# A graph network layer with routed experts: block rows of the tail loaded up to seven steps ahead, last stores on another queue, collects spread wider

## The chip, the cores and the metric

One Trainium2 chip, one of its cores. The engines are TensorE (PE, with its weight loads as PEld), VectorE (DVE), ScalarE (ACT), GpSimd (POOL) and SyncE (SP, which here only issues transfers). The metric is the time of one execution on the device in microseconds, as the median of several runs.

## The reference, cut to what matters

The layer has 6250 nodes of 256 float32 values and 200000 edges sorted by destination.

```python
edge_index = jnp.stack([src, dst])
xn = _layernorm(x, axis=-1)
x = x + gnn(xn, edge_index, W, att_src, att_dst, bias) + mix(xn[None], ...)[0]
x = x + ffn(_layernorm(x, axis=-1)[None], gamma, beta, Wr, br, W1, b1, W2, b2)[0]
```

`gnn` is graph attention with four heads: every edge weighs its source's row by a softmax over the edges of one destination, and the rows are summed per destination. `mix` is linear attention over all nodes followed by a two-layer product with a gelu. `ffn` is what the change touches: each node picks two of eight experts by its logits, each expert is 256 -> 512 -> 256 with a gelu between, and the two results are summed with the softmax of the two logits as weights:

```python
logits = xn @ Wr + br
top_vals, top_idx = jax.lax.top_k(logits, 2)
w = jax.nn.softmax(top_vals, axis=-1)
for e in range(8):
    h = jax.nn.gelu(xn @ W1[e] + b1[e], approximate=False)
    y = y + (h @ W2[e] + b2[e]) * w_full[..., e, None]
```

## The kernel before, in words

**Steps.** All engines walk through one plan of 211 numbered steps, each engine with its own program and semaphores between them. A step up to 168 (`NS` = 169) carries one group of 1024 edges: GpSimd gathers the source rows into `rows_g`, VectorE builds a one-hot matrix `pick_e` (two places, 128 x 8 x 128 float32 each) and weighs the rows, TensorE multiplies them (`sums`, L2366) and signals `summed`. Beside this, each step carries pieces of the other work. From step 169 on only that other work is left; this is the tail. SyncE's loop runs with a lag of five passes, so that its step `c` is named like the others' steps.

**Routing.** The 49 tiles of 128 nodes are finished in the order 48 down to 0. Tile t is routed at step `route_at[t]` (tile 1 at 169, tile 0 at 170): its row is normed, its logits are computed (L2460, L1841), its two experts chosen, and its rows written to `sent_dram`, where each expert has a region. Tiles 48 to 24 are scattered by GpSimd. Tiles 23 to 0 are sorted by expert with a product (`sort`, L2479), stored in `sorted_dram` (`keep_sorted`, L1416) and then handed out to the regions, two experts to a piece (`hand_out`, L1430, on SyncE). The tiles 10, 5, 1 and 0 are rushed: half of their pieces is handed out by ScalarE (`hand_out_rest`, L2212 to L2214), for tile 1 in ScalarE's step 179 and for tile 0 in its step 180.

**Sets and blocks.** The tiles form four sets: 48 to 24, 23 to 10, 9 to 5, and 4 to 0. When a set is routed, `table` writes which blocks of 128 rows it has and whose expert each is (`table_ready`). The sets have 42, 43, 17 and 17 blocks. At the end of the last three sets the regions are filled up with zeros (`fills`, L1454: eight transfers of 384 KB), which must come after the hand-outs before it and ahead of those of the next tile. `fill_at` gives the step, 176 for the last set; its second term, the end of the hand-outs before, is below that.

**One block** is one job. The jobs of the third set stand at steps 167 to 183, those of the last set at 184 to 200. Job n at step s goes through: load of its rows by SyncE at step s-3 (`block_inputs`, L1384) into one of the two places of `xe` (the buffer `xin`), after the turn of job n-2; turn by TensorE at step s-1 (`turn_x`, L2376); taken to `xnT` by ScalarE (L2144), which at step s also copies the expert's first weights to `W1_now` (L2156); up product at step s (L2404, sixteen matmuls); gelu by ScalarE (L2171); down product at step s+2 (`down`, L2442 for the bias and then L2444, eight matmuls); copy from PSUM into one of the two places of `ys` (the buffer `xn`) by VectorE at step s+3 (`result`, L1793), which must wait until the store of job n-2 has landed (`ys_out`); and store to `set_dram`. Up to job step 168 the store is SyncE's at step s+3 (L1393); from 169 on (`LATE`) it is ScalarE's at step s+4 (L2227). In TensorE's program a step reads: turn of the next job, sums, sort products, down product of the job two steps back (after VectorE's copy of the job before that one), up product.

**The end of a tile.** When all blocks of a span of sets (the first two sets, then each by itself) are stored, each tile is collected: GpSimd gathers its two result rows per node from `set_dram` (`collect`, L1577, two gathers of 128 KB), SyncE reloads the kept sum for tiles from 9 on (`x1_again`, L1463, at step `final_at[t]`), VectorE adds both with their shares (`combine`, L1977 and L1980, at `final_at[t]` + 2, for the last set + 4), and SyncE stores the rows of the output (`give`, L1468, one step later). There are six places for this (`TAIL_SPOTS`) in the freed `rows_g`: collect and reload of the f-th tile wait for the sum of the tile six before. `final_at` begins at 171 and gives two tiles to each step, up to 193 for tile 5 (summed at 195); the last set's five tiles stand at 204 and 205.

Of the kernel before, what the change touches and what calls it, by code (L numbers as in the profile page):

```python
# [10 lines left out]
P = 128  # L11
# [24 lines left out]
WINDOWS = 8  # L36
NEAR = 6
CUTS = (24, 10, 5)
CLOSED = (1, 2, 3)
TAIL_RATE = 3  # L40
COLLECT_RATE = 2
TAIL_SPOTS = 6
SPARE_F = 8
PADDED = 1 << 14
# [4 lines left out]
TURNED = 14  # L49
XR = 14  # L50
SORT_BUFS = 8
BY_TWO = 2


def gps_layer(nc, x, xT, src_cols, dst_cols, W_turned, att_cols, inner_cols, src, dst, gnn_W, att_src, att_dst, gnn_bias, w_qkv, b_qkv, kln_g, kln_b, vln_g, vln_b,
# [3 lines left out]
    NT = -(-N // P)  # L59
# [15 lines left out]
    NE, _, H = W1.shape  # L75
# [10 lines left out]
    sent_dram = nc.dram_tensor("sent_dram", (NE * REGION + max(SPARE, SPARE_F) * P, D), F32).ap()  # L86
# [14 lines left out]
    SETS = tuple(zip((FULL,) + tuple(c - 1 for c in CUTS), CUTS + (0,)))  # L101
# [4 lines left out]
    NS = NG - COUNTED  # L106
    LATE = NS
# [6 lines left out]
    def steps_until(t):  # L114

        return min(NS, NG - int(NG * math.sqrt(P * t / N)) + 2)

    mix_first = PAIRS + 5
    mix_at, route_at, table_at, final_at = {}, {}, [], {}
    for t in range(FULL, -1, -1):  # L120
        mix_at[t] = mix_first + FULL - t
    for t in range(FULL, -1, -1):
        at = max(steps_until(t), mix_at[t] + 8)
        if t == 0:
            at = max(at, pair_at[-1] + 2)
        if t < FULL:
            at = max(at, route_at[t + 1] + 1)
        if t + 3 <= FULL:
            at = max(at, route_at[t + 3] + (4 if t + 3 >= CUTS[0] else 6))
        if t + 2 < CUTS[0]:  # L130
            at = max(at, route_at[t + 2] + 3)
        if any(t == hi for hi, _ in SETS[1:]):
            at = max(at, table_at[-1] - 4, mix_at[0] - 3)
# [20 lines left out]
    SORTED = tuple(range(SETS[0][1] - 1, -1, -1))  # L154
    HANDS = NE // BY_TWO
    RUSHED = tuple(t for t in SORTED if any(t == lo for _, lo in SETS[1:]) or route_at[max(t - 1, 0)] < route_at[t] + HANDS and t - 1 in (lo for _, lo in SETS[1:]))
# [4 lines left out]
        piece_at_step[c] = waiting[:now] + [(t, k) for t in RUSHED if route_at[t] + 9 == c for k in range(HANDS // 2)]  # L161
        waiting = waiting[now:]
    handed_at = {t: c for c, gone in piece_at_step.items() for t, _ in gone}
    fill_at = {x: max(route_at[SETS[x][1] + 1] + 7, handed_at[SETS[x][1] + 2] + 1) for x in CLOSED}
    assert all(fill_at[x] <= min(c for c, gone in piece_at_step.items() if SETS[x][1] + 1 in dict(gone)) for x in CLOSED)
    downs_dram = nc.dram_tensor("downs_dram", (3 * NE, D), BF16).ap()
    sorted_dram = nc.dram_tensor("sorted_dram", (SORT_BUFS, 3 * P, D), F32).ap()
    set_dram = [nc.dram_tensor(f"set_dram{w}", (span_blocks[w] * P, D), F32).ap() for w in range(len(spans))]

    job_at, job_step, mix_number, last_job = {}, {}, {}, []  # L170
# [4 lines left out]
    for z in range(len(SETS)):  # L175
        at = max(table_at[z] + (7 if z else 4), max(job_at) + (1 if z else 4))
        for k in range(set_blocks[z]):
            job_at[at + k] = (len(job_step), "block", z, k)
            job_step[len(job_step)] = at + k
        last_job.append(len(job_step) - 1)  # L180
    xe_count = {}
    for n, kind, _, _ in job_at.values():
        same = [m for m, other, _, _ in job_at.values() if m <= n and m % 2 == n % 2]
        kinds = {m: other for m, other, _, _ in job_at.values()}
        xe_count[n] = sum(1 for m in same if kinds[m] == "block")
    tiles_in = [range(hi, lo - 1, -1) for hi, lo in SETS]
    span_tiles = [[t for x in range(a, b + 1) for t in tiles_in[x]] for a, b in spans]
    for w, (_, z) in enumerate(spans):
        ends = z == len(SETS) - 1
        at = max([job_step[last_job[z]] + (4 if ends else 5)] + [c + 1 for c in final_at.values()])  # L190
        for f, t in enumerate(span_tiles[w]):
            final_at[t] = at + f // (TAIL_RATE if ends else COLLECT_RATE)
    assert spans[-1][0] == spans[-1][1] and min(final_at.values()) >= NS
    final_number = {t: f for f, t in enumerate(final_at)}
    assert max(final_at[t] for t in final_at if t not in tiles_in[-1]) < job_step[last_job[-1]] + 4
# [12 lines left out]
    turn_number = {}  # L208
# [25 lines left out]
    with ExitStack() as ctx:  # L234
# [7 lines left out]
        ident = sb("ident", [P, P])  # L242
# [843 lines left out]
        _, loop_sem = last_phase.enter_context(phase())  # L1086
        loop_marks = []

        def loop_stage(ph):
            def sem(name):  # L1090
                loop_marks.append(loop_sem("loop_" + name))
                return loop_marks[-1]

            rows_g = sb("rows_g", [P, RING, EG, HW_], c=ph)
            pick_e = sb("pick_e", [P, SLOTS, EG, P], c=ph)
# [44 lines left out]
            blk_expert = sb("blk_expert", [1, P], I32, c=ph)  # L1140
            cuts = sb("cuts", [1, SORT_BUFS, 2, NE], I32, c=ph)
            xe, ys = xin, xn
            freed = acc[:, SETS[0][1]:NT].rearrange("p t c -> p (t c)")
            cells = lambda lo, n: freed[:, lo:lo + n]
            bias_parts = cells(H // 2, D // 2).bitcast(BF16)
# [81 lines left out]
            ps_pick, ps_sum, ps_xT, ps_hT, ps_up, ps_small = psA[0], psB, psA[1], psC[0], psC[1], psD[1]  # L1227
# [8 lines left out]
            local_in, window_in = [sem(f"local_in{r}") for r in range(AHEAD)], [sem(f"window_in{r}") for r in range(WINDOWS)]  # L1236
# [2 lines left out]
                                 "ph_ready", "summed", "added", "ids_set"))  # L1239
            xT_in, xe_in, ys_out = ([sem(f"{n}{u}") for u in range(2)] for n in ("xT_in", "xe_in", "ys_out"))  # L1240
            base_in = [sem(f"base_in{v}") for v in range(4)]
            b_given_in, b_split_ready, b_split_out, bias_in, inner_bias_in, bias_of_ready = (sem("b_" + n) for n in ("given_in", "split", "split_out", "in", "inner_in", "of"))
            up_done, hb_ready, gelu_done, h_turned, hT_ready, down_done, ys_ready = (sem("j_" + n) for n in (
                "up_done", "hb_ready", "gelu_done", "h_turned", "hT_ready", "down_done", "ys_ready"))
            x_turned, xT_taken, weights_taken = sem("x_turned"), sem("xT_taken"), sem("weights_taken")
# [36 lines left out]
            def jobs_with(s):  # L1282
                return job_at[s] if s in job_at else None
# [15 lines left out]
            def sort_number(t):  # L1299
                return SETS[0][1] - 1 - t  # L1300

            def handed_by(t):

                return 16 * BY_TWO * (sort_number(t) + 1)

# [9 lines left out]
            def on_sync(sp):  # L1315
# [50 lines left out]
                def block_inputs(n, x, k):  # L1366
                    b, u = first_block[x] + k, n % 2
                    sp.wait_ge(table_ready, 2 * (x + 1))
                    at = sp.value_load(blk_row[0:1, b:b + 1], min_val=0, max_val=NE * REGION // P + SPARE_F - 1)
                    if k == 0:  # L1370
                        sp.wait_ge(ys_ready, NT)
                        for w in range(3):
                            sp.wait_ge(sent[w], 32 * scattered(w))
                        if x:
                            for piece in range(HANDS):
                                sp.wait_ge(handed[piece], handed_by(SETS[x][1]))
                        if filled_by(x):
                            sp.wait_ge(fills_out, filled_by(x))
                        sp.wait_ge(spare_out, 16 * SPARE_F)
                        sp.wait_ge(x1_first, 16 * FIRST_KEPT)  # L1380
                        sp.wait_ge(x1_out, 16 * (NT - FIRST_KEPT - SETS[0][1]))
                    if ("job", n - 2) in turn_number:
                        sp.wait_ge(x_turned, turn_number[("job", n - 2)] + 1)
                    sp.dma_start(xe[:, u], sent_dram[bass.ds(at * P, P)]).then_inc(xe_in[u], 16)  # L1384

                def store(n, kind, a, k):
                    u = n % 2
# [20 lines left out]
                def keep_sorted(t):  # L1408
                    n = sort_number(t)
                    sp.wait_ge(xT_taken, turn_number[("high", t)] + 1)  # L1410
                    if n == 0:
                        sp.wait_ge(tails_out, 16 * SORT_BUFS)
                    if n >= SORT_BUFS:
                        for k in range(HANDS):
                            sp.wait_ge(handed[k], handed_by(t + SORT_BUFS))
                    sp.dma_start(sorted_dram[n % SORT_BUFS, 0:2 * P].rearrange("(k p) n -> p k n", p=P), sorted_home[n % 2][:]).then_inc(sorted_out[n % 2], 16)  # L1416

# [52 lines left out]
                with sp.If(general_value(sp) == 0):  # L1470
# [7 lines left out]
                    for s in range(STEPS + LAG):  # L1478
# [17 lines left out]
                        c = s - LAG  # L1496
                        for i in range(NT):
                            if i // 2 - 2 == c:
                                kv_inputs(i)
                        job = jobs_with(c + 3)  # L1500
                        if job and job[1] == "block" and job[0] >= NT + 2:
                            block_inputs(job[0], job[2], job[3])
                        job = jobs_with(c - 3)
                        if job and (job[1] == "mix" or c - 3 < LATE):
                            store(*job)
                        job = jobs_with(c + 3)
                        if job and job[1] == "block" and job[0] < NT + 2:
                            block_inputs(job[0], job[2], job[3])
                        job = jobs_with(c + 2)
                        if job and job[1] == "mix":  # L1510
                            mix_inputs(job[0], job[2])
                        job = jobs_with(c + 1)
# [617 lines left out]
            def on_scalar(act):  # L2130
# [151 lines left out]
                with act.If(general_value(act) == 0):  # L2282
# [8 lines left out]
                    for s in range(STEPS):  # L2291
# [47 lines left out]
                        for x in range(len(SETS)):  # L2339
                            if table_at[x] == s:  # L2340
                                exponentials(x)
                        if s - 4 >= LATE and jobs_with(s - 4):
                            store(*jobs_with(s - 4))

            def on_tensor(pe):
# [22 lines left out]
                    last.then_inc(summed, 1)  # L2368

                def turn_x(n):  # L2370
                    u = n % 2
                    pe.wait_ge(xe_in[u], 16 * xe_count[n])
                    if turn_number[("job", n)] > 0:
                        pe.wait_ge(xT_taken, turn_number[("job", n)])
                    for c in range(KT):
                        last = pe.transpose(ps_xT[:, c * P:(c + 1) * P], xe[:, u, c * P:(c + 1) * P], ident[:])  # L2376
                    last.then_inc(x_turned, 1)

                experts = {}
# [1369 lines left out]
```

## Time and profile before

| | us |
|---|---|
| median of 3 runs | 2117.38 (2115.78 to 2124.63) |
| the profiled execution | 2116.04 |
| its span, first to last instruction | 2114.3 |
| TensorE busy | 1766.4 |
| VectorE busy | 1595.4 |
| GpSimd busy | 1454.6 |
| ScalarE busy | 1214.1 |

The mean granted clock of TensorE over the span is 0.902 of its full speed. The shares of busy time are averages over stages of different kinds: the edge loop takes the first nine tenths of the span, and the tail from about 1890 us on has other limits. Rows are therefore read by stretch. Times in rows are in microseconds from the start of the span. Matmul ends are modelled, so the starts of matmuls are the sharper marks. A tile name in a row is the program's name of the buffer, which may hold other data by then: `xin` holds block rows, `xn` finished blocks, `rows_g` in the tail the collected and kept rows, `acc` tables in cells that have become free.

### The profile page before, as it was taken

How to read it: one execution, taken by the hardware profiler on the slowest of the kernel's cores; microseconds unless marked ns; L12 is line 12 of the kernel's file. 1: busy time of each engine (PE TensorE's matmuls, PEld its weight loads, DVE VectorE, ACT ScalarE, POOL GpSimd, SP SyncE). 2: the span in 40 equal slices, each digit the busy share in tenths (PEclk: the TensorE clock that was granted, in tenths of full speed). 3: DMA queues.
4: the chain of work that ended last, by engine and by line, in shares of the span. 5: the costliest groups of instructions: out<-in, count | busy, mean ns of one | idle time of the engine just before them, and what ended most of it. 6: DMA issues, size and time to landing. Idle time of an engine off the chain costs nothing. (4 is left out here: it accounts for less than half of the span.)

```text
span 2114.3 us, 40584 instructions
## 1 busy us (share of the span) xinstructions
PE 1766.4 (84%) x10047; PEld 1433.6 (68%) x10048; DVE 1595.4 (75%) x3938; ACT 1214.1 (57%) x2310; POOL 1454.6 (69%) x1586
## 2 busy tenths in 40 slices
PE   8499999678677777777788989889998999997684
PEld 6367777556555565555677777767877888885574
DVE  7678888567677777779888888979986998865341
ACT  4433333235454554444877787868865898855252
POOL 3277777777777777777766777766777777755451
PEclk9799999888787878778999999999999999998897
DMA  9676665686666666666776777876777778847772
GB/s 333 150 189 173 173 175 154 189 283 184 172 181 180 179 181 180 167 171 165 202 199 195 219 215 210 235 227 170 196 223 226 209 210 203 215 122 231 218 217 70
DMA packets 289175, 411.77 MB, mean 195 GB/s; under 512 B 108855, under 2 KB 211519, under 8 KB 285226
## 3 DMA queue, kind: packets, MB, share of 16 engines
q0 software_dynamic: 74208, 206.08, 36.4%
q1 hardware_dynamic: 194520, 185.22, 29.3%
q10 hardware_dynamic: 20210, 17.79, 2.9%
q8 instruction: 90, 1.47, 0.3%
q14 instruction: 147, 1.20, 0.2%
HBM read 354.61 MB, written 90.98 MB: 211 GB/s over the span
## 5 line engine op out<-in xcount | busy, mean ns | idle before, releaser
L1555 POOL DMA_INDIRECT rows_g<-node_table,src_all x1347 | 1282.6, 952 | 469.9 <-issue 407.9
L2366 PE MATMUL psB<-rows_g,pick_e 128*128 128x260 f32 x2704 | 747.4, 438 | 142.3 <-issue 120.0
L2366 PEld LDWEIGHTS psB<-rows_g,pick_e 128*128 128x128 f32 x2704 | 582.4, 221 | 266.8 <-issue 161.3
L1730 DVE TENSOR_TENSOR rows_g<-rows_g,psD 128x2048 f32<-128x2048 f32 x169 | 384.8, 2277 | 0.0
L2138 ACT ACTIVATE pick_n<-local_row 128x1024 bf16<-128x1024 bf16 x169 | 178.6, 1057 | 174.7 <-PE psA L2355 161.2
L2404 PEld LDWEIGHTS psC<-xnT,W_now 128*128 128x128 f32 x1904 | 233.8, 194 | 9.2 <-ACT W_now L2156 2.6
L2404 PE MATMUL psC<-xnT,W_now 128*128 128x128 f32 x1904 | 234.3, 277 | 1.6 <-ACT W_now L2156 1.6
L1701 DVE TENSOR_TENSOR pick_e<-psD,slot_all 128x1024 f32<-128x1024 f32 x169 | 203.4, 1204 | 0.1
L2134 ACT ACTIVATE local_row<-local_row,minus_id 128x1024 bf16<-128x1024 bf16 x169 | 191.6, 1134 | 15.8 <-DVE both_f L2040 8.7
L1793 DVE COPY xn<-psD 128x256 f32<-128x256 f32 x119 | 50.2, 422 | 179.3 <-DMA set_dram<-xn 97.0
L1577 POOL DMA_INDIRECT rows_g<-set_dram,places x98 | 95.0, 970 | 129.2 <-issue 86.0
L2355 PE MATMUL psA<-window,pick_n 128*128 128x24 bf16 x1352 | 59.5, 174 | 96.8 <-DVE psD L1711 51.3
L2355 PEld LDWEIGHTS psA<-window,pick_n 128*128 128x128 bf16 x1352 | 55.0, 99 | 119.5 <-issue 114.7
L2156 ACT ACTIVATE W_now<-W_f 128x1024 f32 x119 | 125.2, 1052 | 15.2 <-issue 13.9
L1719 DVE TENSOR_TENSOR p_both_e<-rows_g,psD 128x64 f32<-128x64 f32 x169 | 48.7, 288 | 110.2 <-DMA rows_g<-node_table,src_all 103.6
L2444 PE MATMUL psD<-W_f,hidT_more 128*128 x480 | 126.3, 408 | 0.0
L2444 PE MATMUL psD<-W_f,hidT 128*128 x472 | 120.9, 400 | 0.0
L2200 ACT ACTIVATE xdT<-psA 128x256 f32<-128x256 f32 (+1 forms) x49 | 18.9, 385 | 174.8 <-PE psA L2453 174.8
L2144 ACT ACTIVATE xnT<-psA 128x256 f32<-128x256 f32 x119 | 44.4, 373 | 114.7 <-PE psA L2376 98.5
L2444 PEld LDWEIGHTS psD<-W_f,hidT_more 128*128 128x128 f32 x480 | 90.5, 199 | 18.4 <-issue 0.9
L2444 PEld LDWEIGHTS psD<-W_f,hidT 128*128 128x128 f32 x472 | 87.0, 194 | 17.2 <-issue 0.4
L2492 PE MATMUL psC<-W_f,xnT 128*128 128x512 f32 (+1 forms) x196 | 90.0, 602 | 3.5 <-DMA xnT<-in_xT_dram 3.5
(387 smaller groups left out, 2924.0 us busy)
## 6 DMA issues: line engine op xcount, KB each, us to landing
local_row<-local_dram SPq DMA_DIRECT2D x169, 256.0 KB, 4.1
sent_dram<-sorted_dram SPq DMA_DIRECT2D x176, 128.0 KB
rows_g<-node_table,src_all POOLq DMA_INDIRECT x1347
xin<-sent_dram SPq DMA_DIRECT2D x119, 128.0 KB
xnT<-in_xT_dram SPq DMA_DIRECT2D x96, 128.0 KB
set_dram<-xn SPq DMA_DIRECT2D x87, 128.0 KB
sent_dram<-zero_dram SPq DMA_DIRECT2D x24, 384.0 KB
acc<-node_table SPq DMA_DIRECT2D x49, 128.0 KB
```

The lines of the kernel that those rows point to most:

```text
L1555: pool.indirect_dma_start(out=rows_g[:, r, j], out_offset=None, in_=node_table, in_offset=bass.IndirectOffsetOnAxis(ap=src_all[:, g, j:j + ...
L1577: pool.indirect_dma_start(out=final_home(f)[0][0:rows, c], out_offset=None, in_=set_dram[span_of[x]], in_offset=bass.IndirectOffsetOnAxis( ...
L1701: dve.tensor_tensor(pick_e[:, r], ids_here.unsqueeze(1).broadcast_to([P, EG, P]), slot_all[:, g].unsqueeze(2).broadcast_to([P, EG, P]), AL ...
L1730: dve.tensor_tensor(heads, heads, p_here.unsqueeze(3).broadcast_to([P, EG, HEADS, C]), ALU.mult).then_inc(ph_ready, 1)
L2134: act.activation(local_row[:, r], local_row[:, r], ACT.Abs, bias=minus_id[:]).then_inc(away_ready, 1)
L2138: act.activation(pick_n[:], local_row[:, r], ACT.Relu, bias=1.0, scale=-1.0).then_inc(pick_n_ready, 1)
L2156: act.activation(W1_now[:].rearrange("p k n -> p (k n)"), W1_f[:, bass.ds(experts[n], 1)].rearrange("p e k n -> p (e k n)"), ACT.Copy).the ...
L2355: last = pe.matmul(ps_pick[:, j * 6 * HEADS:(j + 1) * 6 * HEADS], pick_n[:, j * P:(j + 1) * P], window[:, w].rearrange("p k a -> p (k a)") ...
L2366: last = pe.matmul(ps_sum[s % 2][:, 0:AW], pick_e[:, s % SLOTS, j], rows_g[:, s % RING, j, 0:AW], start=(j == 0), stop=(j == EG - 1))
L2404: last = pe.matmul(inner_bank(n)[:, c * P:(c + 1) * P], W1_now[:, k, c * P:(c + 1) * P], xnT[:, u, k], start=(k == 0), stop=(k == KT - 1))
L2444: last = pe.matmul(ps_small[:, down_at], turned_rows(n, kind)[:, c], W2_f[:, bass.ds(e, 1), c], start=False, stop=(c == HK - 1))
L2492: last = pe.matmul((ps_up, ps_hT)[u][0:rows, :], xnT[:, u, k, 0:rows], wkv_s[:, k], start=(k == 0), stop=(k == KT - 1))
```

## The change

Three things change.

First, from job 139 (step 172) on, the block rows no longer go through the two places of `xe` but through eight places laid over `pick_e`, which the edge loop no longer needs. The first such load waits for the last `summed`; a load waits only for the turn of the job eight before. Jobs 139 to 143 are all loaded at step 169, the later ones of the third set seven steps ahead of their own, and those of the last set from step 180 on (four at 180, then one per step). Before, each was loaded three steps ahead. They use the semaphores of `window_in` further.

Second, the stores of the last set's blocks (steps 184 to 200) go from ScalarE at step s+4 to SyncE at step s+3. The third set's late stores (steps 169 to 183) stay on ScalarE.

Third, `final_at` of the tiles of the first three sets gives three tiles to two steps and not two to each, so that it runs to 199 and the sums to 201 (before 193 and 195), and the fill term is one step smaller: 175 for the last set, while those of the second and third stay at 116 and 137 by their other term.

```diff
-COLLECT_RATE = 2
+COLLECT_RATE = 3
+LATE_ROWS = 8
-    fill_at = {x: max(route_at[SETS[x][1] + 1] + 7, handed_at[SETS[x][1] + 2] + 1) for x in CLOSED}
+    fill_at = {x: max(route_at[SETS[x][1] + 1] + 6, handed_at[SETS[x][1] + 2] + 1) for x in CLOSED}
+    late_first = next(n for n, (at, kind) in enumerate((job_step[m], job_at[job_step[m]][1]) for m in range(len(job_step))) if kind == "block" and at >= NS + 3)
+    load_at = {n: at - 3 for n, at in job_step.items()}
+    for n in range(late_first, len(job_step)):
+        load_at[n] = max(job_step[n] - LATE_ROWS + 1, NS, route_at[0] + 10 if job_at[job_step[n]][2] == len(SETS) - 1 else 0)
-            final_at[t] = at + f // (TAIL_RATE if ends else COLLECT_RATE)
+            final_at[t] = at + (f // TAIL_RATE if ends else 2 * f // COLLECT_RATE)
...
+            late_rows = pick_e[:].rearrange("p r j n -> p (r j n)").rearrange("p (v c) -> p v c", v=LATE_ROWS)
+            late_spot = lambda n: (n - late_first) % LATE_ROWS
+            job_rows = lambda n: xe[:, n % 2] if n < late_first else late_rows[:, late_spot(n)]
...
+            late_in = window_in
+            def late_landed(n):
+                v = late_spot(n)
+                return 16 * (sum(1 for s in range(NS) if s % WINDOWS == v) + (n - late_first) // LATE_ROWS + 1)
... (block_inputs on SyncE)
+                    if n >= late_first:
+                        if n == late_first:
+                            sp.wait_ge(summed, NS)
+                        if n >= late_first + LATE_ROWS:
+                            sp.wait_ge(x_turned, turn_number[("job", n - LATE_ROWS)] + 1)
+                        sp.dma_start(job_rows(n), sent_dram[bass.ds(at * P, P)]).then_inc(late_in[late_spot(n)], 16)
+                        return
... (SyncE's loop)
-                        job = jobs_with(c + 3)
-                        if job and job[1] == "block" and job[0] >= NT + 2:
-                            block_inputs(job[0], job[2], job[3])
+                        for n in range(NT + 2, len(job_step)):
+                            if load_at[n] == c:
+                                block_inputs(n, *job_at[job_step[n]][2:])
                         job = jobs_with(c - 3)
-                        if job and (job[1] == "mix" or c - 3 < LATE):
+                        if job and (job[1] == "mix" or c - 3 < LATE or job[2] == len(SETS) - 1):
                             store(*job)
... (ScalarE's loop)
-                        if s - 4 >= LATE and jobs_with(s - 4):
+                        if s - 4 >= LATE and jobs_with(s - 4) and jobs_with(s - 4)[2] < len(SETS) - 1:
                             store(*jobs_with(s - 4))
... (turn_x on TensorE)
-                    pe.wait_ge(xe_in[u], 16 * xe_count[n])
+                    if n < late_first:
+                        pe.wait_ge(xe_in[n % 2], 16 * xe_count[n])
+                    else:
+                        pe.wait_ge(late_in[late_spot(n)], late_landed(n))
-                        last = pe.transpose(ps_xT[:, c * P:(c + 1) * P], xe[:, u, c * P:(c + 1) * P], ident[:])
+                        last = pe.transpose(ps_xT[:, c * P:(c + 1) * P], job_rows(n)[:, c * P:(c + 1) * P], ident[:])
```

## Rows read from the trace of the kernel before

**Rows 1.** Busy time by stretch: start:end, length, engines, granted clock, DMA share, GB/s.
```profile
1914.60:1940.00 25.40, 17.39 (x97) 13.84 (x96) 16.80 (x74) 10.09 (x26) 11.20 (x12) 0.83 0.64 183
1940.00:1963.40 23.40, 18.09 (x84) 14.93 (x83) 10.36 (x32) 8.49 (x17) 11.12 (x13) 0.75 0.87 294
...
2003.60:2035.10 31.50, 25.28 (x164) 21.77 (x163) 13.05 (x31) 17.05 (x42) 24.19 (x25) 1.00 0.84 253
...
2058.80:2089.30 30.50, 28.96 (x177) 24.52 (x176) 3.01 (x8) 15.60 (x39) 0.00 (x0) 1.00 0.20 66
```

**Rows 2.** Waits of TensorE, 1893 to 2092: in total, times, longest.
```profile
PE psD L2442 <- DVE xn L1793: 30.0, 15, 8.4
PE psD L2442 <- DVE logit_f L1841: 4.9, 1, 4.9
```

**Rows 3.** Waits of VectorE, 2003 to 2092.
```profile
DVE xn L1793 <- DMA set_dram<-xn: 56.9, 18, 4.5
```

**Rows 4.** Timeline of TensorE: start, duration, what, idle before it in brackets.
```profile
1893.49 0.28 PE L2442 MATMUL psD<-acc 24*128 24x256 bf16 x1
...
1897.63 0.28 PE L2442 MATMUL psD<-acc 24*128 24x256 bf16 x1
...
1956.78 0.39 PE L2442 MATMUL psD<-acc 24*128 24x256 bf16 x1 [4.48 <-DVE xn L1793]
...
1976.03 0.39 PE L2442 MATMUL psD<-acc 24*128 24x256 bf16 x1 [8.37 <-DVE xn L1793]
...
2003.56 0.28 PE L2442 MATMUL psD<-acc 24*128 24x256 bf16 x1
...
2028.31 0.28 PE L2442 MATMUL psD<-acc 24*128 24x256 bf16 x1
...
2087.02 0.28 PE L2442 MATMUL psD<-acc 24*128 24x256 bf16 x1 [0.77 <-DVE xn L1793]
```

**Rows 5.** Timeline of all engines, 2017 to 2025: one store and who needs it.
```profile
2017.03 0.38 PE L2376 MATMUL psA<-ident,xin 128*128 128x128 f32 x2
...
2018.66 0.33 ACTq L2227 DMA_DIRECT2D set_dram<-xn  x1
...
2023.46 0.42 DVE L1793 COPY xn<-psD 128x256 f32<-128x256 f32 x1 [3.83 <-DMA set_dram<-xn]
...
2024.04 0.28 PE L2442 MATMUL psD<-acc 24*128 24x256 bf16 x1 [1.88 <-DVE xn L1793]
```

**Rows 6.** TensorE grouped by line, 2003.56 to 2028.31, then 2028.31 to 2087.02.
```profile
L2442 PE MATMUL psD<-acc 24*128 24x256 bf16 x5 | 1.4, 276 | 3.7 <-DVE xn L1793 3.7
...
L2442 PE MATMUL psD<-acc 24*128 24x256 bf16 x13 | 3.6, 276 | 6.1 <-DVE xn L1793 5.9
```

**Rows 7.** Transfers by line, KB, median us to landing: 2003 to 2047, then 1936 to 1962.
```profile
rows_g<-x_dram SPq DMA_DIRECT2D x14, 128.0 KB, 3.8
...
rows_g<-x_dram SPq DMA_DIRECT2D x4, 128.0 KB, 7.7
```

**Rows 8.** Timeline of SyncE: the last set's fill.
```profile
1937.92 7.18 SPq L1454 DMA_DIRECT2D sent_dram<-zero_dram  x8
```

**Rows 9.** Timeline of VectorE: the second of tile 1's cut numbers.
```profile
1922.01 0.16 DVE L1877 CAST cuts<-acc 1x8 int32<-1x8 f32 x1
```

**Rows 10.** The chain that ended last, in order of time: start, duration, what.
```profile
1949.75 6.36 DMA set_dram<-xn
...
1957.17 3.71 PE psD L2444 x8
...
1999.70 1.92 PE psD L2444 x8
```

**Rows 11.** Timeline of ScalarE: the hand-outs of tile 1.
```profile
1966.76 6.35 ACTq L2214 DMA_DIRECT2D sent_dram<-sorted_dram  x4
```

**Rows 12.** Line L1577, 2003 to 2047: durations ns, first and last start, landings.
```profile
L1577 POOL DMA_INDIRECT rows_g<-set_dram,places x35: 942/946/1132, 2002.3 to 2045.7; - x35
...
DMA to landing us min/median/max: 2.7/3.9/4.9
```

More of the change, by code:

```diff
@@ L180, in gps_layer @@
         last_job.append(len(job_step) - 1)
+    late_first = next(n for n, (at, kind) in enumerate((job_step[m], job_at[job_step[m]][1]) for m in range(len(job_step))) if kind == "block" and at >= NS + 3)
+    load_at = {n: at - 3 for n, at in job_step.items()}
+    for n in range(late_first, len(job_step)):
+        load_at[n] = max(job_step[n] - LATE_ROWS + 1, NS, route_at[0] + 10 if job_at[job_step[n]][2] == len(SETS) - 1 else 0)
     xe_count = {}
     for n, kind, _, _ in job_at.values():
-        same = [m for m, other, _, _ in job_at.values() if m <= n and m % 2 == n % 2]
+        same = [m for m, other, _, _ in job_at.values() if m <= n and m % 2 == n % 2 and m < late_first]
         kinds = {m: other for m, other, _, _ in job_at.values()}
@@ L1241, in loop_stage @@
             base_in = [sem(f"base_in{v}") for v in range(4)]
+            late_in = window_in
+            assert LATE_ROWS == WINDOWS
+            def late_landed(n):
+                v = late_spot(n)
+                return 16 * (sum(1 for s in range(NS) if s % WINDOWS == v) + (n - late_first) // LATE_ROWS + 1)
             b_given_in, b_split_ready, b_split_out, bias_in, inner_bias_in, bias_of_ready = (sem("b_" + n) for n in ("given_in", "split", "split_out", "in", "inner_in", "of"))
@@ L1381, in block_inputs @@
                         sp.wait_ge(x1_out, 16 * (NT - FIRST_KEPT - SETS[0][1]))
+                    if n >= late_first:
[5 more added lines that the diff above has]
+                        return
                     if ("job", n - 2) in turn_number:
                         sp.wait_ge(x_turned, turn_number[("job", n - 2)] + 1)
-                    sp.dma_start(xe[:, u], sent_dram[bass.ds(at * P, P)]).then_inc(xe_in[u], 16)
+                    sp.dma_start(job_rows(n), sent_dram[bass.ds(at * P, P)]).then_inc(xe_in[u], 16)
                 def store(n, kind, a, k):
@@ L2370, in turn_x @@
                 def turn_x(n):
-                    u = n % 2
-                    pe.wait_ge(xe_in[u], 16 * xe_count[n])
+                    if n < late_first:
+                        pe.wait_ge(xe_in[n % 2], 16 * xe_count[n])
+                    else:
+                        pe.wait_ge(late_in[late_spot(n)], late_landed(n))
                     if turn_number[("job", n)] > 0:
```

## The prediction, made before the change was run

> **What bounds the kernel now.** I read the busy shares by stretch first [rows 1]. The edge loop ends at about 1890 us; the change touches nothing before that point except in name, since up to step 168 every load and store stands where it stood. So all of the gain or loss lies in the 220 us after it. There TensorE works 25.3 of 31.5 us from 2004 to 2035 with the DMA engines at 0.84, and 29.0 of 30.5 from 2059 to 2089 with them at a fifth. From 2089 on (25 us) only the last collects, sums and stores run. The reader should see that TensorE is the engine to follow until 2089 and that it has holes.
>
> Next, who makes the holes. TensorE's idle time ahead of the down product's first matmul (L2442) is 30.0 us on the copy of a finished block into `ys` (tile `xn`, L1793) and 4.9 us on a logit [rows 2]. That copy in turn waits for the store of the block two before it, because `ys` has two places: from 2003 to 2092 that is 56.9 us of VectorE's waiting, and nothing in it is for a block row or for the tail's gathered rows [rows 3]. A turn of block rows (L2376) nowhere waits for its load. So **the loads that are made earlier have nothing of their own to win**; what matters is what becomes free of them on SyncE, and how soon the stores land.
>
> An undisturbed step of one block takes 1897.63 - 1893.49 = 4.14 us, from one L2442 to the next [rows 4]. In the plan's count these are the starts of steps 169 and 170; step 184 starts at 2003.56, step 189 at 2028.31 and step 202, the last, at 2087.02.
>
> **How a store binds** [rows 5]. ScalarE's store of job k-4 comes in its step k, behind the take of the turned rows: turn at 2017.03, store issued at 2018.66, the copy that needed it at 2023.46 after 3.83 us of idling, and the down product at 2024.04, of whose lateness TensorE shows 1.88 us. The landing is thus 4.7 us there. Two steps must hold 3.8 (down to next turn) + 1.6 (turn to issue) + landing + 0.6, so a step is 3.0 us plus half the landing: 4.14 only with a landing under 2.3 us.
>
> **Part 1: the last set's stores on SyncE.** They are jobs of steps 184 to 200. SyncE issues such a store in its step c = job + 3, as soon as the copy is done, which is about 2.8 us after the job's down product began (its nine matmuls' 2.3 and the copy's 0.4); ScalarE did it more than a step later, behind other work. From the copy the next copy of the same place is two steps off, 8.3 us. With 4.7 us of landing and 0.35 for the issue, over 3 us are to spare. The first copy helped is the one of job 186, ahead of step 190. In the thirteen steps from 189 to 202 TensorE idles 6.1 us before L2442, nearly all on that copy [rows 6]. I take all 6.1 as gained. Bounds: 0 (another wait stands behind it) and 7.3 (58.71 us of these steps against ten at 4.14, then 3.9, 3.9 and 2.2 without a turn). If the cover goes, the price is half a microsecond a step for each microsecond of landing beyond the spare 3.
>
> Queued behind SyncE's new wait are, in the same step, the kept rows' load (L1463) and the stores of finished rows (L1468). A step issues a load, a store and one and a half of each of these two, five transfers; at the 0.33 us of a store's issue [rows 5] that is 1.7 us (an estimate), under 4.14. A kept row is wanted two steps after its load: 8.3 us, minus 1 for the issues, minus a median landing of 3.8 in this stretch [rows 7].
>
> The Trainium skill (page "DMA: Bandwidth & Descriptors", section "Issuing engines are not separate DMA queues") says that moving an issue saves only the sequencer's time, since all run on the same engines; by that the landing stays as it is, and the sum stays. Its section "Queues, rings and completion order" speaks against the change: each issuing engine has its own row, a row's descriptors start in order and the engines alternate between rows, so that a store on SyncE stands behind the loads and stores that SyncE issued before it, where ScalarE's row was nearly empty. No row here shows both for one moment; it makes one of the rivals below.
>
> **Part 2: loads ahead, and so an earlier fill.** Every block load before waited on SyncE for a turn (job n-2). With eight places it waits for none, and SyncE is then paced by VectorE's sums, about a step earlier. The first five loads go out together once the last edge sum is done, 2 us of issue; they lie beside TensorE's steps 169 to 171, which have rows already. What moves is the fill of the last set: eight DMAs of 384 KB, 3 MB in all, issued at 1937.92 over 7.2 us [rows 8]. They need the cut numbers, which VectorE has at 1922.2 [rows 9]. The plan puts them one step earlier, and SyncE would be there: I expect the fill at 1922 to 1930. That is 15 us sooner and into a stretch in which the DMA engines are busy 0.64 of the time rather than 0.87 [rows 1].
>
> The burst's price now: kept rows land in 7.7 us and not 3.8 [rows 7], and ScalarE's store of 1949.75 takes 6.36 us; TensorE's down at 1956.78 waited 4.48 us for it and then ran its eight products in 3.71 us where others take 1.92 [rows 4, 10] (the granted clock averages 0.75 in that stretch [rows 1]: part of it at 1.2 and part at 2.4 GHz, the lower after the idling). With a landing of 4.0 (between the undisturbed ones and the 4.7 above) the down starts 2.4 us sooner; its wait is then 2.1 us; after the wait of 1.88 us at 2024.04 the next step began 4.27 us later, nearly undisturbed [rows 4, 5], so 1.8 (the down products) and an estimated 0.6 (the up products behind them) come back: 4.8 us. Bounds: minus 4 (the burst does the same to the two stores that gate steps 176 and 177) and plus 6.9 (the whole wait). I keep 4.8, because steps 175 to 177 are set by the sort products between TensorE and ScalarE, and a store landing 2.6 us later just fits under them.
>
> The two waits after this, the first of them 8.37 us at 1976.03 [rows 4], are not touched: ScalarE's hand-outs of the last two tiles (6.35 us for four [rows 11], and as much again) stand before its stores of set 2, and both stay on ScalarE. SyncE's own hand-outs of these tiles can come 5 to 8 us earlier, which nobody waits for: ScalarE's are last.
>
> **Part 3: three tiles per two steps.** The collects take GpSimd 43.4 us from the first to the last of 35 gathers, so 1.28 us each and 2.55 per tile [rows 12]: 5.1 us per step at two tiles, 3.8 at one and a half. Above 4.14 it would have become the bound as soon as the stores let go; so this part is the cover of part 1. Bytes per step fall from 1.28 MB (two tiles at 512 KB, a block's load and store) to 1.02 MB; at 4.14 us this is 247 GB/s, where 253 were moved [rows 1]. Landing therefore does not grow. The last sums move from step 195 to step 201, two steps before the last block's copy: nothing behind them. For steps 184 to 189, whose stores are still ScalarE's and in which TensorE idles 3.7 us [rows 6], the lighter traffic may take 0.7 to 1 us off a landing, half of it a step: I take 1.2, bounds 0 and 3.7.
>
> **The end** stays: after the last copy the store, five collects, sums and stores, 25 us.
>
> **Sum.** 6.1 + 4.8 + 1.2 = 12.1 us. The profiled execution took 2116.04 us around a span of 2114.3, and is 1.3 below the median of 2117.38. 2116.04 - 12.1 = 2103.9, with the median's offset 2105.3; I say 2104.5.
>
> **Rivals.** (a) *The burst only changes its place*, or SyncE, which now waits for ScalarE's last hand-outs one step earlier, keeps the kept rows behind it: their loads go out near 1988 rather than 1979, wanted at 1992, so a landing of 7.7 us costs 3.8. Either takes the 4.8 away: 6.1 + 1.2 = 7.3, or 2109 to 2110. For it: 3 MB take some 12 us wherever they stand. Against: steps 175 to 177 do not wait for stores now. (b) *All landings shorten*: from 3.9 to the least seen, 2.7 [rows 12], half of it (0.6) per step for about eight of steps 171 to 189 that wait for stores, and the logit's 4.9 us wait (it too stands behind a store's landing) loses 2: 7 us more, 2097. Against it: until 1914 the six first collects go out together as before. (c) *Slower: SyncE ties itself to VectorE.* Copy, store, kept row's load, landing, sum, third copy from there: 3 steps must hold 3.1 us plus the landing. From a landing of 9.3 it exceeds 4.14, from 10.5 the present step (58.71/13 = 4.5), and at 14 a step is 5.7: 15 us lost in these thirteen steps, less what part 2 brings, near 2128. Against it: the kept rows' 7.7 came with the fill under way [rows 7], which is over by then. The order within a row that the Trainium skill states (above) would be what drives it. (d) *It doesn't do what it says*, the last copies waiting for sums whose rows come late: 0 from part 1, so 6 us, 2110; with (a) in what follows.
>
> **Chances.** Forecast 0.52 (its own range 2100 to 2109), (a) and (d) 0.32, (b) 0.10, (c) 0.06. Half a per cent is 10.6 us, about what a measurement can tell from no change: faster means under 2106.8. That holds three quarters of the forecast, a seventh of (a) and all of (b): 0.54; slower 0.06; the same 0.40. The range, 2096 to 2115, takes in (b) and the upper bounds, and leaves (c) out.
>
> **What would show it.** From step 190 on no wait of L2442 on the copy, and steps of 4.1 to 4.2 us; GpSimd pausing between its gathers; the fill near 1922; the down of step 178 waiting about 2 us; the two hand-out waits near 8 and 5 us. Wrong, if a set's copies wait for stores of SyncE, if VectorE waits for kept or gathered rows, or if steps 175 to 177 grow.

## The result, and the profile after

The changed kernel takes 2105.19 us (median of 6 runs, 2102.59 to 2108.22) beside 2117.27 of the kernel before: 12.1 us less by the medians. The ratio is 0.9934 (14.0 us) with a 95% interval of 0.9920 to 0.9947, which is 11.2 to 16.9 us. Forecast were 2104.5 in a range of 2096 to 2115. The profiled execution has a span of 2102.9 us. One execution of the changed kernel, in its third measurement (e9 below), took 4233.47 us, twice the others, and is left out of that measurement's time and ratio.

That profile must be read with care, because its sum is more than what the runs gained. Its step 169 starts at 1900.65 us where the kernel before had 1893.49, though nothing ahead of it was changed; from there to the end it takes 202.3 us against 220.8. Busy time by stretch (columns as in [rows 1]; the stretches are those from the starts of steps 174, 179, 184 and 189 to 202):

```profile
1930.70:1962.90 32.20, 27.67 (x145) 22.27 (x145) 16.62 (x69) 14.18 (x32) 13.88 (x15) 0.86 0.74 239
1962.90:1998.90 36.00, 23.36 (x136) 19.76 (x136) 10.30 (x27) 12.27 (x31) 12.31 (x14) 0.86 0.66 201
1998.90:2022.20 23.30, 20.88 (x136) 18.20 (x136) 9.60 (x23) 12.20 (x30) 15.77 (x17) 1.00 0.83 256
2022.20:2075.70 53.50, 52.52 (x330) 44.16 (x330) 21.70 (x50) 30.38 (x75) 27.46 (x29) 1.00 0.65 198
```

In the last of them TensorE is full. Its waits from 1900 to 2082 (total, times, longest), where [rows 2] had 30.0 and 4.9:

```profile
PE psD L2466 <- DVE xn L1815: 16.2, 9, 8.6
PE psD L2466 <- DVE logit_f L1863: 4.3, 1, 4.3
```

VectorE's from 1992 to 2082, where [rows 3] had 56.9 us on the stores alone. What it waits for now is mostly TensorE, and a line has come that these rows did not have, the kept rows:

```profile
DVE xn L1815 <- PE psD L2468: 35.0, 15, 3.3
DVE xn L1815 <- DMA set_dram<-xn: 12.3, 5, 4.1
DVE rows_g L1999 <- DMA rows_g<-x_dram: 5.4, 2, 3.9
```

One store and its neighbours, timeline of all engines, answering to [rows 5]. The copy waits for the down product, SyncE sends the block 0.45 us after the copy's start and then the finished and the kept rows, and the next down product (2026.79) follows the turn at once:

```profile
2024.40 0.42 DVE L1815 COPY xn<-psD 128x256 f32<-128x256 f32 x1 [1.89 <-PE psD L2468]
...
2024.85 0.32 SPq L1415 DMA_DIRECT2D set_dram<-xn  x1
2025.21 0.91 SPq L1490 DMA_DIRECT2D out_dram<-rows_g  x2
2026.29 0.33 SPq L1485 DMA_DIRECT2D rows_g<-x_dram  x1
...
2026.79 0.28 PE L2466 MATMUL psD<-acc 24*128 24x256 bf16 x1
```

TensorE grouped by line in steps 184 to 189 and 189 to 202, answering to [rows 6]: 3.7 us of idling have become 2.6, and 6.1 have become nothing.

```profile
L2466 PE MATMUL psD<-acc 24*128 24x256 bf16 x5 | 1.4, 277 | 2.6 <-DVE xn L1815 2.4
...
L2466 PE MATMUL psD<-acc 24*128 24x256 bf16 x13 | 3.6, 278 | 0.0
```

The fill on SyncE's timeline and the store that gated step 178 in the chain ([rows 8], [rows 10]). From the start of step 169 the fill comes after 30.7 us, before it was 44.4, and the store lands in 2.0 us and not 6.36. The second cut number ([rows 9]) is there at 1928.65, 2.65 us ahead of the fill:

```profile
1931.30 7.15 SPq L1476 DMA_DIRECT2D sent_dram<-zero_dram  x8
```
```profile
1955.78 2.00 DMA set_dram<-xn
...
1958.73 1.92 PE psD L2468 x8
```

And GpSimd's gathers from 2012 to 2056, answering to [rows 12]: 32 in 43.4 us and not 35, with landings nearly as before.

```profile
L1599 POOL DMA_INDIRECT rows_g<-set_dram,places x32: 942/946/1147, 2011.2 to 2054.6; - x32
...
DMA to landing us min/median/max: 2.8/3.6/4.5
```

### The profile page after: what moved, and what is told of

Its sections match the earlier page's. It is cut to its first block and busy times, and to the rows that moved or that the text cites. A ratio compares the mean times of both kernels' runs of the same rounds, so it can differ in the third digit from the quotient of the medians.

```text
span 2102.9 us, 40583 instructions
## 1 busy us (share of the span) xinstructions
PE 1761.4 (84%) x10047; PEld 1429.2 (68%) x10048; DVE 1595.5 (76%) x3938; ACT 1213.1 (58%) x2310; POOL 1455.5 (69%) x1586
## 3 DMA queue, kind: packets, MB, share of 16 engines
q0 software_dynamic: 74208, 206.08, 36.5%
## 5 line engine op out<-in xcount | busy, mean ns | idle before, releaser
L1577 POOL DMA_INDIRECT rows_g<-node_table,src_all x1347 | 1283.4, 953 | 474.9 <-issue 408.1
L2166 ACT ACTIVATE xnT<-psA 128x256 f32<-128x256 f32 x119 | 44.3, 373 | 98.6 <-PE psA L2400 83.5
```

The costliest lines, as they stand in the source:

```text
L1577: pool.indirect_dma_start(out=rows_g[:, r, j], out_offset=None, in_=node_table, in_offset=bass.IndirectOffsetOnAxis(ap=src_all[:, g, j:j + ...
```

## The experiments

Each was compared with the kernel before on one chip. What follows leans on one table, made from the starts of the down products' first matmul in each profile: microseconds from the start of one step to that of another. The times of a row are from one profile, and there is one profile of the kernel before.

```
                         169-174 174-179 179-184 184-189 189-202  rest | 169 starts | ratio (95%)
before                     30.8    39.2    40.1    24.8    58.7   27.3 |   1893.5   |
changed                    30.1    32.2    35.9    23.3    53.5   27.2 |   1900.7   | 0.9934 (0.9920-0.9947)
e0, changed again          32.8    33.7    37.9    27.3    54.1   28.0 |   1892.4   | 0.9932 (0.9913-0.9952)
e9, changed again          32.1    32.0    36.8    27.7    53.5   27.6 |   1895.5   | 0.9930 (0.9908-0.9951)
e1, stores alone           31.4    37.7    40.6    26.5    52.4   27.3 |   1897.9   | 0.9977 (0.9964-0.9991)
e2, loads ahead alone      31.7    33.1    39.8    28.4    55.7   27.3 |   1900.6   | 0.9967 (0.9954-0.9981)
e3, 3 tiles/2 steps alone  30.7    38.5    37.8    24.8    62.4   27.3 |   1896.1   | 0.9996 (0.9981-1.0011)
e4, changed, fill +7       30.6    32.8    37.4    24.2    53.9   27.3 |   1894.1   | 0.9936 (0.9923-0.9949)
e5, changed, 2 tiles/step  31.4    33.6    40.7    23.8    53.0   27.3 |   1904.6   | 0.9954 (0.9941-0.9966)
e6, before, fill +6        30.0    35.1    40.1    24.2    56.9   27.3 |   1899.3   | 0.9982 (0.9971-0.9992)
e7, all late stores SyncE  32.1    31.7    39.5    20.7    53.5   27.3 |   1896.5   | 0.9925 (0.9906-0.9943)
e8, those from step 177    31.7    32.7    37.3    21.0    52.7   27.5 |   1893.7   | 0.9917 (0.9901-0.9933)
```

**e0, the changed kernel again.** No edit.

> The changed kernel once more. Its first profile gained 18.5 us from the start of step 169 on (2087.02 - 1893.49 = 193.5 us before, 2075.70 - 1900.65 = 175.1 after) and lost 7.2 us ahead of it: 3.4 before 1644 us and 3.6 in step 168, whose sums began late and ran slowly. Theory A: those 7.2 us are scatter of the edge loop, which the change does not touch; then this profile has step 169's start anywhere between 1890 and 1901, the tail again takes 174 to 177 us, and the ratio is 0.9915 to 0.995. Theory B: the change costs them (another program, other code fetches): step 169 starts within 1 us of 1900.6 again.

Step 169 started at 1892.4 us, earlier than in the kernel before, and over all profiles, whatever was changed, it starts between 1892.4 and 1904.6. The 7.2 us are scatter of the edge loop. To the start of step 202 the tail took 185.7 us (2078.11 - 1892.37), where I had said 174 to 177. So a single profile's sum is no measure here, and only stretches that repeat are read from the table.

**e1, the stores alone.**

```diff
 COLLECT_RATE = 2
-if job and (job[1] == "mix" or c - 3 < LATE):            # SyncE
+if job and (job[1] == "mix" or c - 3 < LATE or job[2] == len(SETS) - 1):
-if s - 4 >= LATE and jobs_with(s - 4):                   # ScalarE
+if s - 4 >= LATE and jobs_with(s - 4) and jobs_with(s - 4)[2] < len(SETS) - 1:
```

> The kernel before with one part alone: the last set's stores on SyncE at step s+3; loads three steps ahead, two tiles a step, fill at 176. Theory A (the stores are the bound of steps 189 to 202, and the collects at 5.1 us per two tiles are the next): steps 189 to 195 fall only from 5.1 to about 5.0, because GpSimd's collects then bind, and steps 195 to 202 to the undisturbed 4.1; gain 2 to 4 us. Theory B (the stores alone bind): the full 5 to 6 us.

The ratio is 4.9 us (1.9 to 7.6), and steps 189 to 202 took 52.4 us, the shortest in the table, with two tiles a step. The collects do not bind. VectorE's waits from 2030 to 2092 in this kernel no longer know a store:

```profile
DVE xn L1793 <- PE psD L2444: 40.2, 15, 3.9
```

**e2, the loads ahead alone.** The eight places and `load_at`, with the fill's term at 7, `COLLECT_RATE = 2` and ScalarE's stores.

> One part alone: eight places, loads up to seven steps ahead; stores of the last set on ScalarE, two tiles a step, fill at step 176. SyncE reaches step 176 when VectorE has done its sums of step 175, so the fill should come at about 1934 to 1936 and not 1938: gain 0 to 2 us. Rival (the loads themselves were late, or SyncE's earlier hand-outs shorten steps 179 to 184, which gained 4.2 us in the changed kernel unforeseen): gain 3 to 5 us, seen in steps 179 to 184.

It gains 7.0 us (4.0 to 9.7), more than any other part, and not where the rival said: steps 179 to 184 are unchanged (39.8), steps 174 to 179 fall from 39.2 to 33.1. The fill went out 39.2 us after the start of step 169:

```profile
1939.84 6.76 SPq L1476 DMA_DIRECT2D sent_dram<-zero_dram  x8
```

Theory A expected it 40.5 to 42.5 us after that start (1934 to 1936 where step 169 starts at 1893.49) and put the gain at 2 us at most. With 5 us of the fill most of part 2 was there; e6 moves the fill alone.

**e3, three tiles per two steps alone.**

```diff
-COLLECT_RATE = 2
+COLLECT_RATE = 3
-final_at[t] = at + f // (TAIL_RATE if ends else COLLECT_RATE)
+final_at[t] = at + (f // TAIL_RATE if ends else 2 * f // COLLECT_RATE)
```

> One part alone: three tiles per two steps, all else as before. Less is moved per step, so stores land sooner; ScalarE's stores still bind. Theory A: half of 0.7 to 1 us a step in the steps that wait for a store, 184 to 195, minus what the tiles moved to steps 196 to 201 cost there: gain 1 to 3 us. Rival (lighter traffic does most of what the change brought, as each two steps hold one landing): 5 us or more.

Nothing that can be told from no change (0.9996). The table says why: 2.3 us less in steps 179 to 184, and 3.7 more in 189 to 202, where ScalarE's stores still bind and the collects now last to the end.

**e4, the changed kernel with the fill's term at 7.** One character of `fill_at`.

> The changed kernel with the fill's term back at +7 (step 176). With the loads ahead alone the fill already went out 39.2 us after step 169's start, against 44.4 before and 30.7 and 33.5 in the two profiles of the changed kernel, and steps 174 to 179 took 33.1 us against 39.2 before and 32.2 and 33.7. Theory A (only SyncE's release from the turns counts; 5 us sooner is enough for the store that gates step 178): the same as the changed kernel, 2105, steps 174 to 179 in 33 to 34 us. Rival (the one step in the plan carries the fill's gain): 4 to 5 us slower, 2110, steps 174 to 179 in 37 us or more.

2105.14 us, the changed kernel's time, and steps 174 to 179 took 32.8 us, with the fill 37.2 us after the start of step 169. Within an interval of about 3 us to either side, the step in the plan has no share in the gain once the loads go ahead.

**e5, the changed kernel with two tiles a step.** e3's edit undone.

> The changed kernel with two tiles a step. Theory P (of the prediction: the collects, 5.1 us for two tiles, bind once the stores do not): steps 184 to 195 at 5.1 us each, 6 to 10 us slower than the changed kernel. Rival S (with the stores alone moved and two tiles a step, steps 188 to 198 already took 4.14 us, so the collects do not bind): within 3 us of the changed kernel.

0.9954: about 4.5 us slower than the changed kernel (0.9930 to 0.9936 in four measurements, with e4), though its interval overlaps with theirs; between the two theories in size, and in neither's place. Steps 184 to 202 took 76.9 us, no more than the changed kernel's 76.8 to 81.4, with the collects running at 39 us for 31:

```profile
L1599 POOL DMA_INDIRECT rows_g<-set_dram,places x31: 945/949/1146, 2015.1 to 2053.8; - x31
```

So they are slower than the steps, 5 us for two tiles against 4.14. But the last gather goes out at 2053.8 us, and the last sum starts at 2057.93, before step 195 does (2059.65): the collects end before their delay has grown large. From 2010 to 2062 VectorE's sums waited 1.5 us for them, in two waits, and from the start of step 189 to that of step 201 TensorE has no wait for a copy, with 4.13 to 4.30 us from one step to the next between the starts of steps 190 and 195. What is lost is in steps 179 to 184: 39.8 to 40.7 in the five kernels with two tiles and ScalarE's stores there, 35.9 to 37.9 in the four profiles of the changed kernel and e4, and in e3. At least a part of it stands in one step with a lower granted clock. Busy time of step 181 in the kernel before, in e5 and in the changed kernel:

```profile
1986.90:1993.80 6.90, 6.90 (x27) 5.83 (x27) 4.19 (x13) 0.00 (x0) 3.78 (x4) 0.57 0.53 156
```
```profile
1993.10:2000.00 6.90, 6.90 (x28) 5.79 (x28) 2.99 (x10) 0.00 (x0) 3.79 (x4) 0.58 0.66 183
```
```profile
1985.30:1989.40 4.10, 4.10 (x27) 3.63 (x27) 3.01 (x10) 0.61 (x3) 1.89 (x2) 1.00 0.56 166
```

The same 27 or 28 matmuls at a granted clock of 0.57 or 0.58 (most of it at 1.2 GHz) take 6.9 us, at 1.00 (2.4 GHz) 4.1. Over all profiles but e7, whose waits lie elsewhere, this step took 5.8 to 7.0 us in the five kernels with two tiles (granted clock 0.57 to 0.71) and 4.1 or 5.8 us in those with three (1.00 in the three profiles of the changed kernel, 0.71 in e3, e4 and e8). So the lower clock goes with two tiles, but the wait just ahead does not explain it. TensorE had idled 5.16, 3.26 and 3.13 us before the three stretches shown; in e2 3.01 us stood before 6.95 us at 0.57, and in e3, e4 and e8 1.94 to 2.14 us before 5.82 us at 0.71, shorter waits than those of the changed kernel (2.46 to 3.13). That lighter collects shorten the landings, hence this wait, and so leave the clock up would be a reading, but these waits speak against it, and what sets the clock here is not shown.

**e6, the kernel before with the fill's term at 6.** Only this.

> The kernel before with the fill's term one step smaller and nothing else: SyncE still waits for a turn ahead of every load. Step 175 of SyncE comes about 5 us before its step 176, so the fill should go out near 35 us after step 169's start and not 44. Theory A (what counts is when the 3 MB go out): gain 3 to 6 us, steps 174 to 179 in 33 to 35 us. Rival (the loads, three steps ahead, are now held up by the burst, or the burst meets the stores that gate steps 176 and 177): 0 or slower, those steps at 39 us or more.

3.8 us (1.7 to 6.1), as theory A had it; steps 174 to 179 took 35.1. The fill went out 39.0 us after step 169's start, later than expected: the load just ahead of it on SyncE waited 6.8 us for a turn. This is the run that shows the cause of most of part 2, since it moves the fill and nothing else. The wait of TensorE before step 178 says the same over all profiles. It was 2.62 to 4.48 us where the fill went out 44.3 to 45.5 us after the start of step 169 (the kernel before, e1, e3), 1.58 us here, and 0.20 to 1.13 us in the others. Of these e2 has the fill no earlier than e6 (39.2 us), waits 0.32 us and needs 1.9 us less for steps 174 to 179; whether the loads ahead give that by another way or it is scatter is open, as e0 and e9 differ by 1.7 us there.

**e7, every late block store on SyncE, ahead of its loads.**

```diff
+job = jobs_with(c - 3)
+if job and c - 3 >= LATE:
+    store(*job)
 for n in range(NT + 2, len(job_step)):
     if load_at[n] == c:
         block_inputs(n, *job_at[job_step[n]][2:])
...
 job = jobs_with(c - 3)
-if job and (job[1] == "mix" or c - 3 < LATE or job[2] == len(SETS) - 1):
+if job and c - 3 < LATE:
     store(*job)
...
-if s - 4 >= LATE and jobs_with(s - 4) and jobs_with(s - 4)[2] < len(SETS) - 1:
-    store(*jobs_with(s - 4))
```

> The changed kernel with the third set's late stores (jobs of steps 169 to 183) on SyncE too, each ahead of SyncE's loads of its step. In the changed kernel the two longest waits left are the down products of steps 180 and 181 (8.6 and 3.1 us and a slowed product), for stores that ScalarE issues after its eight hand-outs. Theory A (those waits are the stores' place in ScalarE's program): steps 179 to 184 fall from 36 to 38 us to about 28, gain 6 to 10 us over the changed kernel. Rival (ScalarE's hand-outs hold up its own take of the turned rows and the copy of the weights as well, so TensorE's up products wait in the stores' stead; or SyncE's own hand-outs hold the stores): gain under 3 us, the waits reappear at L2428 or at the same place.

0.9925, by the ratios 1 to 2 us better, which the intervals can't tell from nothing: the gain is as the rival had it. The 12.8 us from the start of step 179 to that of 180 became 4.1, and steps 184 to 189 took the undisturbed 20.7, but the time from the start of step 180 to that of 184 took what was won (35.4 us, where the changed kernel had 23.1). The waits of all engines from 1960 to 2000 name both successors: the kept rows, which SyncE loads behind its hand-outs, and the copy of the weights behind ScalarE's.

```profile
DVE rows_g L2002 <- DMA rows_g<-x_dram: 25.0, 5, 9.1
...
PE psC L2429 <- ACT W_now L2181: 8.1, 2, 4.9
```

This run also bounds what was said of the fill. SyncE, now held by the copies that its stores wait for, sent the fill 42.8 us after the start of step 169, nearly as late as in the kernel before:

```profile
1939.30 6.78 SPq L1476 DMA_DIRECT2D sent_dram<-zero_dram  x8
```

Steps 174 to 179 took 31.7 us even so, and TensorE waited 0.62 us before step 178. Here the store that gates this step goes out behind the fill, at 1947.82, 51.3 us after the start of step 169, where ScalarE had sent it after 56.3 us in the kernel before. So an early fill is one way to have that store land in time, and an earlier store another.

**e8, the same from the job of step 177 on.** `c - 3 >= route_at[0] + 7` on SyncE, the jobs before stay on ScalarE.

> As e7, but SyncE takes over the block stores only from the job of step 177 on; those of 169 to 176 stay on ScalarE. With all of them on SyncE the steps 184 to 189 took the undisturbed 20.7 us (23.3 to 27.3 in the changed kernel), but in steps 179 to 184 VectorE waited 9.1, 8.7 and 6.2 us for kept rows, which SyncE loads behind a store and its hand-outs, and those steps took 39.5 us. Theory A (the two effects separate by where the hand-outs stand): steps 179 to 184 back at 36 to 38 us and 184 to 189 still at 20.7 to 22, gain 2 to 5 us over the changed kernel, 2100 to 2103. Rival (the stores of jobs 177 and 178, now on SyncE, bring the kept rows' delay along): steps 179 to 184 at 39 us or more, no gain over e7.

2103.57 us where the changed kernel had 2106.08 beside it: 0.9917 against 0.9930, whose intervals overlap. Both stretches came as theory A had them (37.3 and 21.0). It is the lowest ratio of all; whether it is faster than the changed kernel is open.

**e9, the changed kernel a third time.** No edit.

> The changed kernel a third time, beside e8 on one chip: 0.9933 of the kernel before. As to its profile: steps 189 to 202 in 53 to 55 us, 174 to 179 in 32 to 34, 179 to 184 in 35 to 38; the start of step 169 anywhere from 1890 to 1905.

0.9930, and the three stretches and the start of step 169 as said.

## Why the prediction was right, point by point

The time came 0.7 us from the forecast, and the two large terms came by the mechanism that was named for them. But all three terms were mis-sized (5.0 us for 6.1, 6.5 for 4.8, and a loss of 0.9 for a gain of 1.2), 3.1 us came where none were forecast, and two claims were wrong. That the number is so close is luck.

- **The stores bind steps 189 to 202, and SyncE frees them: right.** 58.7 us became 53.5 to 54.1 in the four profiles with the change (e4 counted): 5.0 us, where 6.1 were taken. Alone it is 4.9 (e1). Against the one profile of the kernel before this may be too much: e2 and e6, with ScalarE's stores and two tiles a step as well, took 55.7 and 56.9 us, and the eight profiles with SyncE's stores 52.4 to 54.1, so that the means are 3.8 us apart. From 2027 us, within step 190, to 2082 VectorE waits for nothing but TensorE before these copies.
- **The loads have nothing of their own to win, SyncE's freedom has: right.** No turn waited for its load in either profile. e6, which moves the fill alone, gained 3.8 us, and e7 shows that the fill counts by how it lies to one store. Taken were 4.8 us in steps 174 to 179; they lost 5.5 to 7.2. The wait before step 178 shrank from 4.48 to 0.45 us, not to 2.1, since the store landed in 2.0 and not 4.0 us. The products' 3.71 us became 1.92, as said.
- **That the plan's earlier step moves the fill: wrong as to the cause.** e4 does as well without it. The release from the turns brings the fill 5 us forward without it (e2), and so does the plan's step without the release (e6); either was enough for most of the gain. The fill came 30.7 to 33.5 us after the start of step 169 in the three profiles of the changed kernel, and 1922 to 1930 were 28.5 to 36.5.
- **Three tiles per two steps as the cover of part 1, because the collects would bind at 5.1 us a step: wrong.** e1 and e5 ran undisturbed steps with two tiles. The step of the working that failed took a rate for a bound without asking how much delay gathers before the last sum is due: about 1 us a step for the few steps up to 195. e5 shows it: 31 gathers in 39 us, 1.5 us of waiting for them.
- **1.2 us from lighter traffic in steps 184 to 189: not found.** 23.3 to 27.7 us against 24.8. Nor did 1.2 follow from its own working, which is half of 0.7 to 1 us in each of five steps, 1.8 to 2.5. The gain of three tiles lies in steps 179 to 184, 2.3 to 4.2 us, where I had said that nothing changes. The two waits on the hand-outs, put near 8 and 5 us, were 8.64 and 3.13 in the first profile after, and the step behind them ran at the full clock. e5 prices the third part at about 4.5 us beside the other two, e3 at 0.8 alone.
- **The sum, right by errors that cancel, which is luck.** Means of the four profiles with the change against the one before: 0.6 us more in steps 169 to 174, 6.5 less in 174 to 179, 3.1 less in 179 to 184, 0.9 more in 184 to 189, 5.0 less in 189 to 202 and 0.2 more at the end, 12.9 in all. Forecast were 0, 4.8, 0, 1.2, 6.1 and 0.
- **The end stays: right**, 27.2 to 28.0 against 27.3 us.
- **The rivals.** (a) fell, as steps 174 to 179 gained, and (d), as steps 189 to 202 did; (b) too: its shorter landings came in one place only. (c), SyncE tied to VectorE, didn't come in steps 189 to 202. VectorE did wait for kept rows, which I had named as a sign of being wrong, but only three times from 1900 us on (7.2 us; before once, 1.9 us), all before 2003 us. The tie itself showed in e7, where VectorE waited 25.0 us for kept rows. The Trainium skill ("DMA: Bandwidth & Descriptors", section "Queues, rings and completion order") says that each issuing engine's row takes its descriptors in order. What that costs a store is not shown here: with nothing else under way the last store is followed by the first collect 2.6 us after its issue, on SyncE (2078.39 to 2080.97) as on ScalarE (2089.7 to 2092.30). Under load no row shows a store's landing on SyncE, because nobody waits for it.

Open is what the third part is worth and by what way: about 4.5 us beside the other two parts, 0.8 alone, with intervals of 3 us and more. The parts measured alone sum to 4.9 + 7.0 + 0.8 = 12.7 us and the whole gained 13.6 to 14.9 by its ratios, so they add up within their intervals; the first two sum to 11.9, and together, in e5, they gained 9.7 (7.2 to 12.5).

## What to carry to other kernels

When a load is made earlier and nobody waited for it, look at what stands behind it on its queue: here a wait removed on SyncE let a 3 MB burst go 5 us sooner, out of the way of a small store that gated the matrix engine (e2), and sending the store earlier did as well (e7). An engine's rate above the step's is a bound only once the delay it gathers exceeds the slack of who waits for it; count the steps before paying for relief. And take a change's terms from stretches that repeat over profiles, since here two executions of one program differ by 11.5 us in a tail of some 210.

## What the runs showed that I had not expected

The start of step 169 scatters by 12 us over twelve profiles (1892.4 to 1904.6), while from the start of each step to the next, from step 152 to 160, all of them take the same to 0.02 us; the differences come in single steps, such as the 7.6 to 11.9 us between the starts of steps 167 and 168, which hold step 168's sums. And a wait of 3.13 us left TensorE's clock at 1.00 where one of 3.26 was followed by 0.58, so that two nearly equal waits stand before steps of 4.13 and 6.89 us. Waits of 1.94 to 2.14 us stood before 5.82 us at 0.71, so the length of this wait does not order the steps. What else differed ahead of them was not isolated.
